# A cross-attention and graph kernel: the first batch's rows are loaded through another engine's queue, and earlier in it

## The chip, the cores and the metric

One Trainium2 chip, one core of it. The metric is the device time of one execution in microseconds (us). TensorE (PE) multiplies matrices, VectorE (DVE), ScalarE (ACT) and GpSimd (POOL) work on elements, and the sync engine (SP) issues transfers. ScalarE can issue transfers too. All transfers of a core are carried by the same 16 DMA engines; SP and ScalarE each feed them through a queue of their own (q1 and q10 in this profile).

## The reference

Four stages follow one another. Here they are in the program's terms, for 4 batches of 256 rows of 512:

```
# L0, an update of low rank, with a_sum made of the context's rows
w     = softmax(x @ router_W.T + router_b)              # 8 mixing weights per row
a_sum = sum over 4 of (x @ ctx.T)                       # 64 columns
x     = nan_to_num(x + 0.5 * sum_n w_n * (a_sum @ lora_B[n].T))
# L1, cross attention with a mask, 32 heads of 16, over the 64 rows of ctx
Q, K, V = x @ Wq.T + bq, ctx @ Wk.T + bk, ctx @ Wv.T + bv
x     = layernorm(x + softmax(mask(Q K.T / 4)) V @ Wo.T + bo) * ln_g + ln_b
# L2 and L3, each four blocks on a graph of the 8 nearest of 512 points
idx   = top_k(-distance(ctx), 8)
for block in range(4):
    p = leaky_relu(x)
    x = (w_c @ p + sum over neighbours of (w_n @ p)) / 9 + x   # w_c = w_n = fside
```

## The kernel before

Weights and x arrive with the contracted dimension first. x of one batch is a tile of 128 partitions by 4 chunks by 256 rows, loaded in two halves of two chunks (256 KB each, semaphores `x0_0` and `x0_1` for batch 0). Products that need precision are made of a high and a low part of each operand, so most operands are split by ScalarE (high part) and VectorE or GpSimd (low part) before TensorE uses them.

Each engine works through an order of steps written out by hand (PE_STEPS, ACT_STEPS, DVE_STEPS, POOL_STEPS, SP_STEPS), in which a step is a kind, a batch and an index. Engines wait for each other by semaphores only. An instruction that waits holds up everything behind it on its engine.

The transfers at the start are not in SP_STEPS. SP issues them in the order of the line LOADS, each through `load` (L442), ahead of all its other steps: mask, ctxT (the context with the contracted dimension first), x0, xyz0, loraB, wk, and so on. ScalarE's block begins with two small transfers of its own, the router's weights (`routerW`, L827, 16 KB) and the router's offset (`rb`, L829, 4 KB), and goes on with ACT_STEPS.

The steps near the start that matter here, by engine:
- VectorE: `fa` (the mask as numbers, and its counts, from `mask_all_i`), `a_ready` (the context's four row groups are added, L1143 and L1144), `fm` (ctx_m, the masked context), `near` (the 8 nearest of a stretch of the graph, L1152 and L1153), `rB` (mix, L1199), `ml` (mixT_lo, L1205).
- TensorE: after 28 warm-up products `lora0` (x_in by a_router; it waits for `a_ready`, `routerW` and each half of x0), `dist0_0`, `router0`, `dist0_1` to `dist0_3` (distances, from xyz and xyz_n), `keys` (ctx_m by wk, waits for `wk`), `adjT0` (L675), `mixed0` (L684), `dist1_0`, `lora1`, `dist1_1`, `ua0` (mixT by loraB).
- ScalarE: `sq0` (L834), `low0` (L872), `lbh` (loraB_hi), `rE0`, `wqh` (wq_hi, L840, waits for `wq`), `sq1` (L834, written to points), `adjC0`, `mh0_0` and `mh0_1` (mixT_hi, L882), `woh`.

Of the kernel before, what the change touches and what calls it, by code (L numbers as in the profile page):

```python
# [14 lines left out]
P = 128  # L15
B, S, H = 4, 256, 512
# [3 lines left out]
KC = H // P  # L20
# [17 lines left out]
BANK = 512  # L38
WARM_UP = 14
POOL_LN = ()  # L40
LOADS = "mask ctxT x0 xyz0 loraB wk xyz1 x1 small wq wv wo"

# [88 lines left out]
def xattn_graph_kernel(nc, xT, ctx, ctxT, mask, maskT, fsideT, lora_BT, router_WT, router_b,  # L133
# [28 lines left out]
    with stack:  # L162
# [6 lines left out]
        def under(*tensors):  # L169

            with ExitStack() as early:
                return [sb(name, shape, dt, early) for name, shape, dt in tensors]
# [23 lines left out]
        wk, wv = under(("wk", [P, KC, H], F32), ("wv", [P, KC, H], F32))  # L196
# [45 lines left out]
        def fb(name, shape, dt=F32):  # L242
            return sb(name, shape, dt, front)
# [4 lines left out]
        x_in = [fb(f"x_in{k}", [P, KC, S]) for k in range(2)]  # L248
# [9 lines left out]
        x1 = fb("x1", [P, KC, S])  # L258
# [5 lines left out]
        small = fb("small", [P, 8])  # L264
# [18 lines left out]
        loads = {}  # L283
# [156 lines left out]
        def _(sp):  # L440
            def load(dst, src, name):
                sp.dma_start(dst, src).then_inc(loads[name], 16)  # L442

            def chunks(w):
                return w.rearrange("(c p) n -> p c n", p=P)

            def load_x(b):
                src = xT.rearrange("(c p) (b s) -> b p c s", p=P, b=B)[b]
                for c in range(0, KC, 2):
                    load(x_in[b % 2][:, c:c + 2], src[:, c:c + 2], f"x{b}_{c // 2}")  # L450

            def load_xyz(b):
                load(xyz[b][0:V, :], ctx[b], f"xyz{b}")
                load(xyz_n[b][0:V, :], ctx[b], f"xyz{b}")

            def load_first(name):
                if name == "ctxT":
                    load(ctx_t[:], chunks(ctxT), name)
                elif name == "mask":
                    src = mask.rearrange("b v -> (b v)").unsqueeze(0).broadcast_to([P, B * V])  # L460
                    load(mask_all_i[:], src, "mask_all")
                elif name in ("x0", "x1"):
                    load_x(int(name[1:]))
                elif name in ("xyz0", "xyz1"):
                    load_xyz(int(name[3:]))
                elif name == "loraB":
                    load(loraB_raw[:], chunks(lora_BT), name)
                elif name == "wk":
                    load(wk[:], chunks(WkT), name)
                elif name == "wq":  # L470
                    load(wq_raw[:], chunks(WqT), name)
                elif name == "wv":
                    load(wv[:], chunks(WvT), name)
                    load(bv_all, bv.unsqueeze(0).broadcast_to([P, H]), "bv")
                    for half in range(2):
                        load(mask_col_i[half * V:(half + 1) * V, :], maskT, "mask_col")
                elif name == "wo":
                    load(wo_raw[:], chunks(WoT), name)
                    load(g_all[:], ln_g.unsqueeze(0).broadcast_to([P, H]), "ln")
                    load(b_all[:], ln_b.unsqueeze(0).broadcast_to([P, H]), "ln")  # L480
                elif name == "small":
                    load(bk_col[:], bk_cols, "bk")
                    load(bq_col[:], bq_cols, "bq")
                    sp.dma_start(bo_col[:], bo.rearrange("(c p) -> p c", p=P), allow_slow_non_contiguous=True)\
                        .then_inc(loads["bo_col"], 16)

            for name in LOADS.split():
                load_first(name)
# [335 lines left out]
        @block.scalar  # L824
        def _(act):

            act.dma_start(a_router[:, :, R:R + NE], router_WT.rearrange("(c p) n -> p c n", p=P))\  # L827
               .then_inc(loads["routerW"], 16)
            act.dma_start(rb_all[:], router_b.unsqueeze(0).broadcast_to([P, NE])).then_inc(loads["rb"], 16)  # L829
# [518 lines left out]
```

## Time and profile before

| | |
|---|---|
| median of 3 runs | 391.87 us (391.63 to 392.79) |
| the profiled execution's own time | 391.98 us |
| its span | 390.2 us |
| busy PE / PE weight loads | 372.0 us (95%) / 311.5 us (80%) |
| busy DVE | 279.2 us (72%) |
| busy ACT | 181.1 us (46%) |
| busy POOL | 127.6 us (33%) |
| moved by DMA | 22.60 MB, mean 58 GB/s |

The span runs from the first to the last instruction that the profiler recorded; 1.8 us of the execution's own time lie outside it. Busy shares are of the span. DMA shares in the tables are the mean busy share of the 16 DMA engines; values a little above 1 occur.

### The profile page before, as it was taken

Reading aid. Unit: us, or ns where it says so; the run is one execution under the profiler, and the core shown is the slowest. Engines: PE = TensorE matmul, PEld = TensorE weight load, DVE = VectorE, ACT = ScalarE, POOL = GpSimd, SP = SyncE. Lnnn points to the kernel's source line nnn. Section 1 sums busy time; section 2 is a strip of 40 time slices with the busy share of each in tenths; the row PEclk is TensorE's granted clock in tenths of the full one; section 3 lists DMA queues with packets and bytes.
Section 4 is the critical chain, followed back from the end, with each engine's and each line's share of the span. In section 5 each row is a group of like instructions: output and inputs, shape, how many; then the busy total and the mean of one; then the engine's idle time right before and its main releaser. Section 6 shows DMA issues by size and latency. Waiting matters only on the chain.

```text
span 390.2 us, 6603 instructions
## 1 busy us (share of the span) xinstructions
PE 372.0 (95%) x2428; PEld 311.5 (80%) x2428; DVE 279.2 (72%) x418; ACT 181.1 (46%) x308; POOL 127.6 (33%) x120
## 2 busy tenths in 40 slices
PE   5799997989999989998999999999999999999996
PEld 5476796776886866986869889888889889988995
DVE  5847859578679876676779877846777866786634
ACT  1357536748529776337735334333333334423410
POOL 7656020400200132203414745333435243523300
PEclk9999999999999999999999999999999999999999
DMA  7992416206435505300000000000000000000022
GB/s 176 299 380 77 127 38 149 61 2 125 86 110 125 113 2 114 89 7 2 2 2 2 0 0 2 0 2 2 0 3 0 2 0 0 3 2 0 2 108 108
DMA packets 25198, 22.60 MB, mean 58 GB/s; under 512 B 9552, under 2 KB 20688, under 8 KB 25168
## 3 DMA queue, kind: packets, MB, share of 16 engines
q1 hardware_dynamic: 24496, 22.17, 20.8%
q8 instruction: 20, 0.33, 0.4%
q10 hardware_dynamic: 672, 0.02, 0.1%
q14 instruction: 10, 0.08, 0.1%
HBM read 12.48 MB, written 3.15 MB: 40 GB/s over the span
## 4 chain that ended last, share of the span: by engine, by line
PE 80%; DMA 6%; DVE 4%; SPq 4%; ACT 3%; issue 2%; POOL 0%; ACTq 0%; DVEq 0%; POOLq 0%
PE slot L561 78%; DMA wk<-in_WkT 3%; SPq L493 2%; ACT probT L966 2%; DMA fs_raw<-in_fsideT 1%; DVE shift L1240 1%; DMA q_stack<-shiftT 1%; SPq L522 1%; SPq L442 1%; PE slot L684 1%; PE slot L675 1%; ACT L966 1%; DVE x L1223 1%; DVE x L1225 0%; PE slot L716 0%
## 5 line engine op out<-in xcount | busy, mean ns | idle before, releaser
L1055 POOL TENSOR_TENSOR p_lo<-p_full,p_hi 128x512 fp32r<-128x512 f32 x64 | 87.1, 1371 | 128.9 <-ACT p_hi L1006 128.8
L1006 ACT ACTIVATE p_hi<-p_full 128x512 fp32r<-128x512 f32 x64 | 39.9, 630 | 73.0 <-DVE p_full L1302 73.0
L561 PE MATMUL slot<-adj,u_hi 128*128 128x512 f32 x256 | 69.2, 395 | 0.0
L561 PE MATMUL slot<-adj,u_lo 128*128 128x512 f32 x256 | 68.5, 394 | 0.0
L1307 DVE TENSOR_TENSOR u_lo<-slot,u_hi 128x512 fp32r<-128x512 f32 x64 | 42.9, 686 | 34.5 <-ACT u_hi L1016 33.9
L1302 DVE SCALAR_TENSOR_TENSOR p_full<-points 128x512 f32<-128x512 f32 x64 | 63.1, 1003 | 3.3
L561 PE MATMUL slot<-fs_hi,p_hi 128*128 128x256 f32 x256 | 63.8, 283 | 0.5 <-ACT probT L966 0.5
L561 PE MATMUL slot<-fs_lo,p_hi 128*128 128x256 f32 x256 | 63.7, 282 | 0.0
L1312 DVE SCALAR_TENSOR_TENSOR points<-slot,points 128x512 f32<-128x512 f32 x64 | 43.5, 687 | 23.5 <-PE slot L561 23.3
L1016 ACT ACTIVATE u_hi<-slot 128x512 fp32r<-128x512 f32 x64 | 37.4, 597 | 44.2 <-PE slot L561 43.7
L561 PEld LDWEIGHTS slot<-adj,u_lo 128*128 128x128 f32 x256 | 45.9, 189 | 9.1 <-issue 1.3
L561 PEld LDWEIGHTS slot<-adj,u_hi 128*128 128x128 f32 x256 | 45.7, 188 | 8.7 <-issue 0.9
L561 PEld LDWEIGHTS slot<-fs_hi,p_hi 128*128 128x128 f32 x256 | 48.7, 190 | 2.0 <-ACT probT L966 1.0
L561 PEld LDWEIGHTS slot<-fs_lo,p_hi 128*128 128x128 f32 x256 | 48.7, 190 | 0.6
L561 PEld LDWEIGHTS slot<-fs_hi,p_lo 128*128 128x128 f32 x256 | 39.5, 189 | 6.7 <-issue 1.9
L561 PE MATMUL slot<-fs_hi,p_lo 128*128 128x256 f32 x256 | 44.2, 285 | 0.0
L1055 POOL TENSOR_TENSOR q_lo<-q_full,q_hi 128x512 fp32r<-128x512 f32 x8 | 10.4, 1308 | 76.0 <-DMA q_stack<-q_lo 53.6
L966 ACT ACTIVATE probT<-slot,mask_col 128x1024 f32<-128x1024 f32 x16 | 17.7, 1114 | 12.9 <-PE slot L561 12.9
L1240 DVE TENSOR_REDUCE shift<-slot 128x16 f32<-128x1024 f32 x16 | 19.3, 1216 | 5.4 <-PE slot L561 5.4
L1152 DVE MAX8 top<-slot 128x8 f32<-128x512 f32 x16 | 11.1, 695 | 10.0 <-PE slot L561 9.9
L933 ACT ACTIVATE k_blk_hi<-kT_hi,half_col 32x256 fp32r<-32x256 f32 x32 | 14.4, 497 | 1.8 <-PE slot L561 1.4
L561 PE MATMUL slot<-x_hi,wq_hi 128*128 128x256 f32 x64 | 14.2, 304 | 1.0 <-issue 1.0
(138 smaller groups left out, 567.5 us busy)
## 6 DMA issues: line engine op xcount, KB each, us to landing
q_stack<-q_hi SPq DMA_DIRECT2D x32, 128.0 KB, 2.8
x_in<-in_xT SPq DMA_DIRECT2D x8, 256.0 KB, 5.5
q_stack<-q_lo SPq DMA_DIRECT2D x16, 128.0 KB, 2.7
out_points<-points SPq DMA_DIRECT2D x8, 256.0 KB, 2.0
loraB_raw<-in_lora_BT SPq DMA_DIRECT2D x1, 1024.0 KB, 9.5
wk<-in_WkT SPq DMA_DIRECT2D x1, 1024.0 KB, 12.7
wq_raw<-in_WqT SPq DMA_DIRECT2D x1, 1024.0 KB, 10.8
wv<-in_WvT SPq DMA_DIRECT2D x1, 1024.0 KB, 11.6
```

The source lines that it names most:

```text
L493: sp.dma_start(q_stack[PART * part:PART * (part + 1), j::HC // 2, :].bitcast(F32), q[PART * j:PART * (j + 1)].bitcast(F32)).then_inc(signa ...
L561: return pe.matmul(dst, lhsT, rhs, start=start, stop=stop, skip_group_check=True)
L933: act.activation(k_blk_hi[rows, :, 2 * j + a, :], kT_hi[rows, :, b * V:(b + 1) * V].bitcast(F32), ACT.Copy, scale=half_col[rows, a:a + 1]) ...
L966: act.activation(probT[:, i % 2, :], both_banks("w", b, i)[:], ACT.Exp, bias=mask_col[:, b:b + 1], scale=QK_SCALE).then_inc(prob_ready, 1)
L1006: act.activation(p_hi[b][:, (i % 2) * H:(i % 2 + 1) * H], p_full[:, p_buf[b, i]], ACT.Copy)\
L1016: act.activation(half_of(u_hi[:, u], i % 2), bank("wa", b, i // 2, i % 2), ACT.Copy)\
L1055: pool.tensor_tensor(lo[:, cut], full[:, cut], hi[:, cut].bitcast(F32), ALU.subtract)\
L1152: link(dve.max(top8[:, i], tile))
L1240: dve.tensor_reduce(pairs, both_banks("sc", b, i)[:].rearrange("p (j a v) -> p j a v", a=2, v=V), AX_X, ALU.max, negate=True).then_inc(max ...
L1302: dve.scalar_tensor_tensor(p_full[:, p_buf[b, i]], pts, SLOPE, pts, ALU.mult, ALU.max)\
L1307: dve.tensor_tensor(half_of(u_lo[:, u], i % 2), bank("wa", b, i // 2, i % 2), half_of(u_hi[:, u], i % 2).bitcast(F32), ALU.subtract).then_ ...
L1312: dve.scalar_tensor_tensor(pts, bank("ga", b, i // 2, i % 2), 1.0 / (TOPK + 1), pts, ALU.mult, ALU.add).then_inc(points_ready, 1)
```

## The change

The two halves of x0 leave SP's list, and ScalarE's block issues them before its two router transfers. Same source, same destination, same sizes, same semaphores.

```diff
-LOADS = "mask ctxT x0 xyz0 loraB wk xyz1 x1 small wq wv wo"
+LOADS = "mask ctxT xyz0 loraB wk xyz1 x1 small wq wv wo"
...
-                elif name in ("x0", "x1"):
-                    load_x(int(name[1:]))
+                elif name == "x1":
+                    load_x(1)
...
         @block.scalar
         def _(act):
 
+            first_rows = xT.rearrange("(c p) (b s) -> b p c s", p=P, b=B)[0]
+            for c in range(0, KC, 2):
+                act.dma_start(x_in[0][:, c:c + 2], first_rows[:, c:c + 2]).then_inc(loads[f"x0_{c // 2}"], 16)
             act.dma_start(a_router[:, :, R:R + NE], router_WT.rearrange("(c p) n -> p c n", p=P))\
                .then_inc(loads["routerW"], 16)
             act.dma_start(rb_all[:], router_b.unsqueeze(0).broadcast_to([P, NE])).then_inc(loads["rb"], 16)
```

On SP, at the very start of the program, the issues stand as follows, with - what was there before and + what is there now (x_in is the tile of x0, xyz and xyz_n are the two copies of the first batch's context):

```order
 L442 DMA mask_all_i<-in_mask 128x256
 L442 DMA ctx_t<-in_ctxT 128x4x256
-L442 DMA x_in<-in_xT 128x2x256 x2
 L442 DMA xyz<-in_ctx 64x512
 L442 DMA xyz_n<-in_ctx 64x512
```

Two issues are gone, and everything behind them on SP moves up by two places.

On ScalarE, at the start of its block, these rows stood before (points holds the router's weights, as a_router):

```order
L824 UNCONDITIONAL_BRANCH
L827 DMA points<-in_router_WT 128x4x8
L829 DMA rb_all<-in_router_b 128x8
L834 ACT_TABLE_LOAD
L834 ACTIVATE xyz_n<-xyz_n 64x512
L872 ACTIVATE low<-slot 72x256
```

and these stand there now:

```order
L824 UNCONDITIONAL_BRANCH
L829 DMA x_in<-in_xT 128x2x256 x2
L830 DMA points<-in_router_WT 128x4x8
L832 DMA rb_all<-in_router_b 128x8
L837 ACT_TABLE_LOAD
L837 ACTIVATE xyz_n<-xyz_n 64x512
L875 ACTIVATE low<-slot 72x256
```

The two halves of x0 come first, and the router's weights and offset, the table load and `sq0` follow two issues later. Nothing else moves on any engine; line numbers behind the new lines are higher by 3.

## Rows read from the trace of the kernel before

**Rows 1.** The page: the span, and DMA's share in 40 slices.

```profile
span 390.2 us, 6603 instructions
...
DMA  7992416206435505300000000000000000000022
```

**Rows 2.** The chain of work that ended last: start us, us, what.

```profile
1.71 0.51 SPq L442
...
2.26 0.47 SPq L442
...
4.74 12.68 DMA wk<-in_WkT
...
17.46 7.17 PE slot L561 x32
...
25.53 0.88 PE slot L684 x8
```

**Rows 3.** The timeline, transfers being issued: start us, us, engine, line, out<-in.

```profile
0.80 0.46 ACTq L827 DMA_DIRECT2D points<-in_router_WT  x1
0.80 0.39 SPq L442 DMA_DIRECT2D mask_all_i<-in_mask  x1
...
1.29 0.52 ACTq L829 DMA_DIRECT2D rb_all<-in_router_b  x1
...
1.84 1.28 ACT L834 ACT_TABLE_LOAD   x1 [1.84 <-issue]
```

**Rows 4.** Windows: PE, PEld, DVE, ACT, POOL, PEclk, DMA share, GB/s.

```profile
1.00:2.00 1.00, 0.42 (x2) 0.42 (x3) 0.94 (x2) 0.16 (x1) 0.62 (x4) 1.00 0.06 17
2.00:3.00 1.00, 1.00 (x6) 1.00 (x6) 0.06 (x1) 1.00 (x1) 0.72 (x6) 1.00 0.39 65
3.00:4.00 1.00, 1.00 (x7) 1.00 (x6) 0.00 (x0) 0.12 (x1) 0.80 (x4) 1.00 0.67 85
4.00:5.00 1.00, 1.00 (x7) 1.00 (x7) 0.00 (x0) 0.00 (x0) 0.74 (x8) 1.00 0.93 200
...
16.00:17.00 1.00, 0.00 (x0) 0.00 (x0) 1.00 (x2) 0.00 (x0) 1.00 (x2) 1.00 1.10 207
```

**Rows 5.** DMA in short windows: transfers' us to landing, and a queue's packets.

```profile
ctx_t<-in_ctxT SPq DMA_DIRECT2D x1, 512.0 KB, 5.9
points<-in_router_WT ACTq DMA_DIRECT2D x1, 16.0 KB, 4.9
...
x_in<-in_xT SPq DMA_DIRECT2D x1, 256.0 KB, 7.4
...
q10 hardware_dynamic: 253, 0.01, 6.8%
```

**Rows 6.** The timeline ahead of keys: start us, us, engine, line, idle before.

```profile
5.53 0.98 DVE L1156 TENSOR_SCALAR attended<-mask_all_i 128x256 f32<-128x256 int32 x1 [3.41 <-DMA mask_all_i<-in_mask]
...
9.54 1.95 PE L561 MATMUL slot<-x_in,points 128*72 128x256 f32 x8 [2.94 <-DVE points L1144]
...
11.20 0.63 ACT L834 ACTIVATE xyz_n<-xyz_n 64x512 f32<-64x512 f32 x1 [8.07 <-DMA xyz_n<-in_ctx]
...
12.98 2.79 PE L561 MATMUL slot<-xyz_n,xyz 128*128 128x512 f32 x6
```

**Rows 7.** The timeline behind keys, from 20 to 30 us, on four engines.

```profile
20.95 1.41 DVE L1199 SCALAR_TENSOR_TENSOR mix<-slot,small,lge 128x512 f32<-128x512 f32 x2
...
23.18 1.91 ACT L840 ACTIVATE wq_hi<-wq_raw 128x2048 fp32r<-128x2048 f32 x1 [7.21 <-DMA wq_raw<-in_WqT]
...
25.11 0.63 ACT L834 ACTIVATE points<-points 64x512 f32<-64x512 f32 x1
...
26.25 1.02 PE L561 MATMUL slot<-points 128*128 128x512 f32 x2
...
28.72 1.28 DVE L1205 TENSOR_TENSOR mixT_lo<-slot,mixT_hi 128x512 fp32r<-128x512 f32 x2
...
29.62 0.39 PEld L561 LDWEIGHTS slot<-mixT_hi,loraB_hi 128*128 128x128 f32 x2 [0.47 <-DVE mixT_lo L1205]
```

## The prediction

> **What bounds the kernel now.** I read the chain of waits first, since only what lies on it can move the end. It starts with SP's issues, one behind the other, goes through the transfer of wk, issued at 4.74 us and landed 12.68 us later at 17.42, and then through TensorE: keys from 17.46, mixed0 at 25.53 [rows 2]. The two issues of x0 are links of that chain, 0.51 and 0.47 us long at 1.71 and 2.26. Next to 12.68 us of transfer the issues are small, so the second question is what the transfer waits for. The windows answer it: in the microseconds from 1 to 5 the DMA engines' share is 0.06, 0.39, 0.67, 0.93, and while wk is under way it is full, 1.10 at 16 to 17 us [rows 4]; the page's digits of 9 for the second and third slice (9.8 to 29 us) say that it stays so [rows 1]. wk therefore does not land a fixed time behind its issue. It lands when everything in front of it has been moved, and the same holds for wq, wv and wo behind it. The stretch of loads is limited by bytes, except for its first few microseconds, where the DMA engines lack work.
>
> Third, what lies beside the chain up to 30 us, as this says how much may come late and what must come early too. Ahead of keys, VectorE starts at 5.53 when the mask lands, and its chain (attended, left_out, counts, the sum of the context) releases lora0 at 9.54; the square of xyz_n starts at 11.20 when xyz_n lands; TensorE's last distances run from 12.98 for 2.79 us, to 15.77 [rows 6]. Then TensorE has nothing until 17.46: 1.69 us of slack. Behind keys, ScalarE sits idle 7.21 us until wq lands, makes wq_hi from 23.18 to 25.09 and the square for batch 1 from 25.11 to 25.74; TensorE's distances that read it start at 26.25, 0.51 us later; VectorE's mixT_lo at 28.72 releases the LoRA products at 29.62 [rows 7]. So between 17.46 and 29.62 two loads matter: wk directly, and wq by way of ScalarE, with 0.51 us of room. Behind 30 us the remaining loads are in or are issued by waits on other engines' work, and every start is relative to another: a shift at 29.62 is carried to the end one for one.
>
> **The change, part by part.** Removed from SP: two issues, 0.51 + 0.47 us with two pauses of 0.04, that is 1.06 us [rows 2]. xyz, xyz_n, loraB and wk are issued 1.06 us earlier, wk at 3.68. Added on ScalarE: two issues ahead of the router's two, whose own take 0.46 and 0.52 us, the first at 0.80 [rows 3]. So the halves of x0 are issued at about 0.80 and 1.31 rather than 1.71 and 2.26, and routerW, rb and the table load start some 1.0 us later. The table load moves from 1.84 to about 2.9 and ends near 4.2 (1.28 us) [rows 3]; ScalarE's first use of it is at 11.20 [rows 6], 7 us later, so this costs nothing. If the cover were gone it would cost 1.0 us of ScalarE.
>
> What 1.06 us of earlier issue is worth. The bytes don't change, and nor do their packets. Where the DMA engines are full, an earlier issue buys nothing; it buys the idle share that it fills. From 2 to 5 us that is 0.61 + 0.33 + 0.07 = 1.01 us of all 16 engines [rows 4]. That and the 1.06 us saved on SP are upper bounds for the gain at about the same value. The lower bound is 0: the mask and ctxT (640 KB) were issued by 1.67 us and still did not fill the engines from 2 to 4 us, so what kept them idle is not only a lack of issued work on q1. For a gain speaks that the other queue was moving in the same time, but only the router's pieces: 253 packets of together 0.01 MB from 2 to 4 us, 6.8% of the engines' time [rows 5]. In their place now stand x0's rows of 1 KB, real work. I take a little over half of 1.01 us: 0.6 us. By this, wk lands at 16.8 and wq 0.6 us earlier too, since both wait for the same backlog.
>
> What of it reaches the end. Keys start 0.6 us earlier, if TensorE is free (15.77, yes) and ctx_m is made. mixed0 would start at 24.9 instead of 25.53; the mix that it reads ends at 20.95 + 1.41 = 22.36 [rows 7], 2.5 us of room. The LoRA products start earlier by the smaller of wk's shift and wq's shift plus 0.51. With both at 0.6 it is 0.6. If only wk's landing moved, 0.51 us would be left.
>
> What comes later. x0 now shares the engines with mask and ctxT from the first microsecond. Before, ctxT took 5.9 us from issue to landing and the second half of x0 7.4 us, to 9.66 [rows 5]. If mask and ctxT come later, VectorE's chain slips, behind it lora0, the distances, the eight nearest, the mix. Room for that: 0.34 us in front of the first distances (lora0 ends at 9.54 + 1.95 = 11.49, they also wait for the square, which ends at 11.20 + 0.63 = 11.83 [rows 6]) plus 1.69 us in front of keys, about 2.0 us, or 1.4 us with keys 0.6 us earlier. I expect the mask to slip by less than 1 us: its 128 KB would yield to at most as much of x0, and 128 KB take 0.6 us at the 200 GB/s of 4 to 5 us, 1.5 us at the 85 GB/s of 3 to 4 [rows 4]. It costs nothing in the sum. The router's weights, now behind x0 in their queue, are needed at 9.54; they took 4.9 us before [rows 5]. Issued at about 1.85 they would land near 6.8 by that, and behind x0's last byte at 9 to 10 if they have to wait for it. That too is inside the room.
>
> Does sharing do anything but save issue time? The rows show only that q1 and q10 were both served from 2 to 4 us, the one with large packets, the other with small ones [rows 5]. The Trainium skill, "DMA: Bandwidth & Descriptors", section "Issuing engines are not separate DMA queues", says that transfers of several engines run on the same 16 DMA engines and interleave, and that issuing from more than one saves only the issuing engine's time. By that rule the gain is at most the issue time taken off SP, 1.06 us here; the trace agrees in so far as wk's landing is set by full engines. Its section "Queues, rings and completion order" says that each DMA engine takes its queues in turn, packet by packet; by that x0 would draw level with mask and ctxT and hold them up, which is the rival of a late lora0 below. No row here shows the turns.
>
> The sum: 391.98 us, the profiled execution's own time, minus 0.6 is 391.4. The profiled execution lies 0.11 us above the median of the runs, so against 391.87 the forecast is 391.3 us. Less than 0.3%, 1.2 us, is about what a measurement of this kernel can't tell from no change.
>
> **The rivals.**
> - *Nothing moves* (chance 0.23). The engines' idle share at 2 to 4 us comes from the start-up of transfers and not from missing issues. For it: 640 KB were issued and the share was 0.39. Against it: the second queue held only small pieces. wk lands at 17.4 as before: 391.9.
> - *The two queues together move faster* (0.14). The rate at full share is not constant: 207 GB/s at 16 to 17 us, and 200 at share 0.93 [rows 4]. If x0's rows mix better with others, wk could land 1.69 us earlier or more, until TensorE's own work ends at 15.77. wq would have to come 1.2 us earlier for it to pass ScalarE. Gain 1.2 to 1.7, about 390.4. Against it: that exceeds both upper bounds above, which hold at equal rates.
> - *lora0 comes late, slower* (0.08). The router's weights wait for the whole of x0, to 9.66, and then take their 4.9 us of before: 14.56. lora0 would start 5.0 us late and end at 16.5, behind it the distances and the router, 3.9 us as from 11.83 to 15.77 before, to 20.4, and keys would start at 20.4 instead of 17.46: 2.9 us later, 394.8. It decides from 2.0 us of lateness of lora0 on; a mask that late would do the same. Against it: most of the 4.9 us is start-up and the crowd of that moment, and the router's pieces cost the engines little.
> - *Only wk moves* (0.05, within the forecast's range): wq lands when it did, gain 0.5, 391.4.
>
> **How the numbers follow.** The forecast, a gain of 0.3 to 1.05, has 0.50: 390.8 to 391.6. With the smaller rivals around it, no change within 0.3% has 0.80, made of 0.50, 0.23, 0.05 and a small part of the third; faster by over 0.3% has 0.12, from the rival of the faster queues; slower by over 0.3% has 0.08. The range reaches from 390.3, which takes in most of the faster rival, to 392.4, which takes in no change with its scatter (the runs shown reach from 391.6 to 392.8); left out are the late lora0 and a tenth at most besides.
>
> **What would show it.** Right: in the profile after, SP's issue of wk starts near 3.7 us; DMA's share from 2 to 4 us is clearly above 0.39 and 0.67; wk lands at 16.4 to 17.1; wq_hi starts before 23.18 by a similar amount; the chain of waits still begins with SP, then wk; mixT_lo and the LoRA products are earlier by 0.3 to 1.0 us, and the same shift is seen late in the span. Wrong: a share from 2 to 4 us as before (then nothing moves), a lora0 later than 11.6, or keys that wait for anything but wk. The prediction also fails if the work behind 52 us, where VectorE enters the chain, does not carry the shift one for one.

## The result and the profile after

The change made the kernel slower: 395.88 us median of 6 runs (394.98 to 396.99) against 392.13 us for the kernel before in the same measurement (6 runs), a ratio of 1.0088 with a 95% interval of 1.0072 to 1.0104. Forecast was a small gain, 391.3 us, in a range up to 392.4. The profiled execution was the slowest of the six, 396.99 us with a span of 395.3; its mean granted clock was 0.983, that of the other five 0.990 or 0.991.

The page of the kernel after, its span, TensorE's share, its granted clock and DMA's share in 40 slices:

```profile
span 395.3 us, 6603 instructions
...
PE 376.6 (95%) x2428; PEld 315.5 (80%) x2428; DVE 279.8 (71%) x418; ACT 181.0 (46%) x308; POOL 127.9 (32%) x120
...
PEclk9699999898999999999999999999999999999999
...
DMA  6992426103504612600000000000000000000022
```

The same instructions ran (2428 products, 22.60 MB moved), yet TensorE was busy 4.6 us longer. The clock's row says why: it has a 6 in the second slice and an 8 in two later ones. The row of before had nines throughout:

```profile
PEclk9999999999999999999999999999999999999999
```

By the windows the fall in the second slice alone (0.60, 0.50, 0.50 and 0.69 from 10 to 18 us) makes a mean of 0.991 over the span. As an estimate from that, the other five executions had this fall and not the two later ones.

The chain of waits after (start us, us, what) begins in another place:

```profile
1.26 8.74 DMA ctx_t<-in_ctxT
...
10.03 0.70 DVE scratch L1146
...
10.75 0.44 DVE points L1147
11.19 2.52 issue
13.71 4.52 PE slot L561 x10
...
28.78 0.88 PE slot L684 x8
```

Before, it went through wk and then keys [rows 2]; now it goes through ctxT, VectorE's two sums and lora0. The 2.52 us called issue are a wait that this view doesn't name. mixed0 (L684) starts at 28.78 instead of 25.53, 3.25 us later. The timeline of the same stretch (start us, us, engine, line, idle before) shows the parts:

```profile
0.80 0.98 ACTq L829 DMA_DIRECT2D x_in<-in_xT  x2
...
1.81 0.49 ACTq L830 DMA_DIRECT2D points<-in_router_WT  x1
...
4.13 0.83 SPq L442 DMA_DIRECT2D wk<-in_WkT  x1
...
11.87 0.63 ACT L837 ACTIVATE xyz_n<-xyz_n 64x512 f32<-64x512 f32 x1 [6.72 <-DMA xyz_n<-in_ctx]
...
13.71 3.66 PE L561 MATMUL slot<-x_in,points 128*72 128x256 f32 x8 [6.17 <-issue]
...
20.81 7.07 PE L561 MATMUL slot<-ctx_m,wk 128*128 128x256 f32 x32
...
24.91 1.91 ACT L843 ACTIVATE wq_hi<-wq_raw 128x2048 fp32r<-128x2048 f32 x1 [4.95 <-DMA wq_raw<-in_WqT]
```

lora0 starts at 13.71 instead of 9.54 and takes 3.66 us instead of 1.95 [rows 6]. What it waited for is found in the DMA view (us from issue to landing), taken in short windows: the second half of x0, ctxT, the router's weights, wk, and last the packets of ScalarE's queue from 9.6 to 13.6 us:

```profile
x_in<-in_xT ACTq DMA_DIRECT2D x1, 256.0 KB, 8.3
...
ctx_t<-in_ctxT SPq DMA_DIRECT2D x1, 512.0 KB, 8.7
...
points<-in_router_WT ACTq DMA_DIRECT2D x1, 16.0 KB, 11.8
...
wk<-in_WkT SPq DMA_DIRECT2D x1, 1024.0 KB, 14.7
...
q10 hardware_dynamic: 170, 0.01, 3.2%
```

x0's second half was issued half-way through the 0.98 us from 0.80 and landed at about 9.6, where it landed before (9.66). ctxT landed at 10.0 instead of 7.2. The router's 16 KB, issued at 1.81, landed at 13.6, which is lora0's start: 11.8 us for a transfer that took 4.9 [rows 5]. wk, issued at 4.13, landed at 18.8 instead of 17.42. So with lora0 on time keys would still have begun 1.4 us late: of their 3.35 us, 2.0 lie beyond wk's landing. Windows (PE, PEld, DVE, ACT, POOL, PEclk, DMA share, GB/s):

```profile
2.00:3.00 1.00, 1.00 (x6) 1.00 (x6) 0.06 (x1) 0.00 (x0) 0.72 (x6) 1.00 0.13 40
3.00:4.00 1.00, 1.00 (x7) 1.00 (x6) 0.00 (x0) 0.14 (x1) 0.80 (x4) 1.00 0.48 165
4.00:5.00 1.00, 1.00 (x7) 1.00 (x7) 0.00 (x0) 1.00 (x1) 0.75 (x8) 1.00 0.72 249
...
7.00:12.00 5.00, 0.54 (x5) 0.35 (x3) 3.25 (x8) 0.13 (x1) 4.43 (x7) 0.84 1.09 218
...
12.00:13.00 1.00, 0.00 (x0) 0.00 (x0) 0.96 (x2) 0.50 (x1) 0.66 (x1) 0.50 1.06 376
```

More bytes were moved from 3 to 4 us than before (165 GB/s, was 85), but the engines' share from 2 to 5 us fell, from 0.39, 0.67 and 0.93 to 0.13, 0.48 and 0.72 [rows 4]. From 7 to 12 us fewer bytes were moved at an unchanged share. Before, the same stretch reads:

```profile
7.00:12.00 5.00, 2.02 (x9) 1.17 (x9) 4.79 (x10) 0.78 (x2) 4.43 (x7) 1.00 1.07 276
```

218 GB/s were moved instead of 276, so 0.1 MB more from 2 to 5 us was followed by 0.3 MB less. Of the packets of this stretch 451 had under 512 bytes, before 58, and ScalarE's queue took 12.2% of the engines' time. Why full engines move fewer bytes isn't shown. And TensorE's clock, after TensorE had stood still since 7.5, was granted at 0.50, the lower of its two levels (1.2 of 2.4 GHz).

### The profile page after: what moved, and what is told of

Same layout as the page of the kernel before. It is cut to its first block, busy times and chain, and to the rows that moved or that the text cites. A ratio compares the mean times of both kernels' runs of the same rounds, so it can differ in the third digit from the quotient of the medians.

```text
span 395.3 us, 6603 instructions
## 1 busy us (share of the span) xinstructions
PE 376.6 (95%) x2428; PEld 315.5 (80%) x2428; DVE 279.8 (71%) x418; ACT 181.0 (46%) x308; POOL 127.9 (32%) x120
## 2 busy tenths in 40 slices
DMA packets 25198, 22.60 MB, mean 57 GB/s; under 512 B 9552, under 2 KB 20688, under 8 KB 25168
## 3 DMA queue, kind: packets, MB, share of 16 engines
q10 hardware_dynamic: 1216, 0.55, 0.5%
## 4 chain that ended last, share of the span: by engine, by line
PE 83%; DMA 5%; SPq 3%; DVE 3%; ACT 3%; issue 2%; POOL 0%; ACTq 0%; DVEq 0%; POOLq 0%
PE slot L561 81%; DMA ctx_t<-in_ctxT 2%; SPq L493 2%; ACT probT L969 1%; DMA fs_raw<-in_fsideT 1%; DMA q_stack<-shiftT 1%; SPq L522 1%; PE slot L675 1%; PE slot L684 1%; DVE shift L1243 1%; ACT L969 1%; DVE x L1228 0%; PE slot L716 0%; ACT fs_hi L993 0%; DVE x L1226 0%
## 5 line engine op out<-in xcount | busy, mean ns | idle before, releaser
L561 PE MATMUL slot<-x_hi,wq_hi 128*128 128x256 f32 x64 | 15.0, 318 | 1.0 <-issue 1.0
## 6 DMA issues: line engine op xcount, KB each, us to landing
loraB_raw<-in_lora_BT SPq DMA_DIRECT2D x1, 1024.0 KB, 11.2
```

Source lines behind the costliest of these rows:

```text
L561: return pe.matmul(dst, lhsT, rhs, start=start, stop=stop, skip_group_check=True)
```

## Experiments

Ratios are to the kernel before, in the runs of the same measurement. Spans and starts are of one profiled execution each; before's is 390.2 us.

**1. The router's weights first.**

```diff
+            act.dma_start(a_router ...routerW)
+            act.dma_start(rb_all ...rb)
             for c in range(0, KC, 2):
                 act.dma_start(x_in[0][:, c:c + 2], ...)
-            act.dma_start(a_router ...routerW)
-            act.dma_start(rb_all ...rb)
```

> The changed kernel with ScalarE's four issues in another order: router's weights, router's offset, then the two halves of x0. Theory A (the loss is the router's pieces standing behind x0 in their queue): the weights land near 6 us as before, lora0 starts when ctxT and VectorE allow, near 11.2 instead of 13.7; the distances end before wk lands (18.8), keys start near 18.9 instead of 20.8; time 2 to 3 us below the changed kernel, near 393.5. Theory B (the loss is x0 sharing the engines from the start, whatever the router does): lora0 and keys start as in the changed kernel, time near 395.9.

Measured: 392.64 us, ratio 0.9983 (0.9964 to 1.0002), span 391.3. The loss is gone. The timeline:

```profile
9.70 1.05 PE L561 MATMUL slot<-x_in,points 128*72 128x256 f32 x4 [3.11 <-DMA x_in<-in_xT]
...
11.66 1.86 PE L561 MATMUL slot<-x_in,points 128*72 128x256 f32 x4 [0.90 <-DMA x_in<-in_xT]
...
17.87 7.07 PE L561 MATMUL slot<-ctx_m,wk 128*128 128x256 f32 x32
```

The router's weights landed 4.7 us after their issue, as before. lora0 began at 9.70, earlier than theory A had it, since more than the weights changed: x0 is now issued behind ctxT, which landed at 7.65 instead of 10.0, and VectorE's sums were done by 9.5. So this run takes away two causes at once, the late weights and the late ctxT; theory B, in which the order on ScalarE does nothing, is out. Now x0 is the late one; its second half landed at 11.6, 2.0 us later than from the sync engine's queue, though issued within 0.1 us of the same time. wk, issued at 3.69, landed 13.2 us later at 16.9, 0.5 us earlier than before. That would be the gain that the prediction had named, but in run 7, with the same loads, wk landed at 17.4; a difference of 0.5 us is what two profiles of the same loads show. lora0's split and a clock of 0.50 in part of 12 to 16 us held TensorE, and keys began 0.4 us later than before.

**2. 28 warm-up products instead of 14**, all else as in the change. The numbers are those of WARM_UP; the trace counts two products for each.

> The changed kernel with 28 warm-up products instead of 14, so that TensorE is busy until about 13.5 us and has no gap in front of lora0. Theory A (part of the loss is TensorE's clock, granted at 0.5 from 10.3 to 17.1 us after TensorE stood still from 7.5 to 13.7): the clock stays at 1.00, lora0 takes 1.95 us instead of 3.66, keys start near 18.9 (wk's landing), time 1.7 to 2.5 us below the changed kernel. Theory B (the clock is a side effect, keys wait for something else): lora0 is shorter but keys start at 20.8 as before and the time is that of the changed kernel, 395.9. If the clock also falls later (68 and 92 us) because of the early gap, these falls vanish too; if not, they stay.

Measured: 395.91 us, ratio 1.0065 (1.0037 to 1.0092). The test needed a busy TensorE until 13.5 us, and the number of products was mis-sized:

```profile
1.58 8.81 PE L561 MATMUL slot<-ident 128*128 128x128 f32 x56 [1.58 <-POOL ident L1027]
...
13.18 3.60 PE L561 MATMUL slot<-x_in,points 128*72 128x256 f32 x8 [2.79 <-issue]
```

The products ended at 10.4, 2.8 us stayed empty, and lora0 took 3.60 us all the same. Inconclusive on the clock; repeated as 6.

**3. The router's weights laid out in memory as one row of 128 bytes for each partition.** This was to give the transfer 128 pieces instead of 512. The tile that it writes stays as it was, with the router's 8 columns at the end of each of 4 chunks, 32 bytes at a time.

```diff
-            act.dma_start(a_router[:, :, R:R + NE], router_WT.rearrange("(c p) n -> p c n", p=P))\
+            act.dma_start(a_router[:, :, R:R + NE], router_WT)\
...
-        "router_WT": a["L0_xattn_router_W"].T,
+        "router_WT": a["L0_xattn_router_W"].T.reshape(KC, P, NE).transpose(1, 0, 2),
```

> The changed kernel with the router's weights laid out in memory as one row of 128 bytes for each partition, so that the transfer has 128 pieces instead of 512. Order of issues unchanged. Theory A (the weights are late because many small pieces behind x0 wait their turn between full-sized pieces of the other queue): they land at least 1.5 us earlier than 13.6, near 10 to 11.5, and lora0 starts with ctxT's chain, near 11.2. Theory B (the lateness is a fixed start-up or x0's place in front): they land near 13 us or later, and the time stays at 395.9.

Measured: 396.30 us, ratio 1.0071 (1.0048 to 1.0094). From issue to landing, and the packets of the whole profile:

```profile
points<-in_router_WT ACTq DMA_DIRECT2D x1, 16.0 KB, 11.5
...
DMA packets 25198, 22.60 MB, mean 57 GB/s; under 512 B 9552, under 2 KB 20688, under 8 KB 25168
```

11.5 instead of 11.8 us, but the page of the change has the same 25198 packets, 9552 of them under 512 bytes, and the same 1216 in ScalarE's queue. The new layout did not lessen the pieces, so this run tests neither theory, and whether fewer pieces would land earlier stays open. It is of use as a second kernel that runs like the change.

**4. The router's transfers held back, x0 left with the sync engine** (kernel before).

```diff
+            loaded(act, "ctxT")
             act.dma_start(a_router[:, :, R:R + NE], router_WT.rearrange("(c p) n -> p c n", p=P))\
```

> The kernel before, with ScalarE's two router transfers issued only once ctxT has landed (7.2 us), x0 staying with the sync engine. Nothing stands in front of the router's pieces in their queue. Theory A (pieces of 32 bytes are slow whenever the other queue keeps the engines full): from issue to landing 4 us or more, landing at 11.5 or later, lora0 late by 2 us or more. Theory B (they are slow only behind x0 in the same queue): landing within 2.5 us, at 9.7, lora0 about as before and time 392.1.

Measured: 399.58 us, ratio 1.0166 (1.0124 to 1.0208). The timeline's lora0:

```profile
16.49 3.30 PE L561 MATMUL slot<-x_in,points 128*72 128x256 f32 x8 [9.60 <-DMA points<-in_router_WT]
```

The DMA view of 10 to 11 us, in which ScalarE's queue is absent as from 7 us on, that of 11 to 12 us, in which it appears for the first time, and the transfer's time to landing:

```profile
q1 hardware_dynamic: 177, 0.36, 102.9%
...
q1 hardware_dynamic: 197, 0.39, 104.2%
q10 hardware_dynamic: 38, 0.00, 2.4%
...
points<-in_router_WT ACTq DMA_DIRECT2D x1, 16.0 KB, 9.4
```

Issued at 6.99 with nothing ahead of it in its queue, the transfer moved no packet before 11 us and landed at 16.4. So it isn't x0 in front that it takes: this transfer was late with nothing in front of it, while the other queue kept the DMA engines full (103 to 109% from 7 to 12 us). That the sync engine's queue would have been faster at that moment isn't shown: wk, issued there at 4.65, landed at 17.5, behind this transfer.

**5. The router's transfers in the sync engine's queue, behind x0** (kernel before).

```diff
-LOADS = "mask ctxT x0 xyz0 loraB wk xyz1 x1 small wq wv wo"
+LOADS = "mask ctxT x0 router xyz0 loraB wk xyz1 x1 small wq wv wo"
...
+                elif name == "router":
+                    load(a_router[:, :, R:R + NE], router_WT..., "routerW")
+                    load(rb_all[:], router_b..., "rb")
```

> The kernel before, with the router's two transfers issued by the sync engine right behind x0, and none by ScalarE. The pieces are the same 640 small ones, behind the same x0, but in the queue that carries the large transfers. Theory C (what is late is the second queue, which gets little of full DMA engines): the weights land near 9.9 us, just behind x0's second half, lora0 starts at 10 to 10.5, keys with wk near 18, time 392 to 393. Theory D (small pieces are late in either queue once the engines are full): they land at 12 us or later, and lora0 with them, time 394 or more.

Measured: 392.54 us, ratio 0.9984 (0.9970 to 0.9997).

```profile
points<-in_router_WT SPq DMA_DIRECT2D x1, 16.0 KB, 7.2
```

Issued at 2.77, later than in the change, the same 512 pieces behind the same x0 landed at 9.97, and lora0 started at 10.01. Theory C holds: neither x0 ahead nor small pieces are enough to make the weights late, and in the second queue they are. Whether small pieces are delayed more there than large ones, no run separates; x0's large halves took 1.1 and 1.9 us longer there in run 1.

**6. 43 warm-up products**, all else as in the change.

> The changed kernel with 43 warm-up products, enough to last until about 13.5 us (28 lasted only until 10.4, and TensorE's clock was still granted at 0.5 from 13 to 17 us). Theory A (the clock is a part of the loss of its own): no 0.5 before 20 us, lora0 takes 1.95 us, keys start at wk's landing, 18.4 to 18.9, time 1.7 to 2.4 us below the changed kernel, 393.5 to 394.2. Theory B: keys start at 20.2 to 20.8 all the same and the time stays at 395.9.

Measured: 393.76 us, ratio 1.0023 (1.0008 to 1.0037), span 392.0, clock 1.000 for the whole span.

```profile
13.61 1.89 PE L561 MATMUL slot<-x_in,points 128*72 128x256 f32 x8
...
18.95 7.07 PE L561 MATMUL slot<-ctx_m,wk 128*128 128x256 f32 x32
```

lora0 is as late as in the change and keys begin 1.9 us earlier. The change's ratio was 1.0088 in its own measurement; with the gap filled 0.65 points of it are gone, some 2.5 us. That compares two measurements; runs 2 and 3, which kept the clock's fall, stood at 1.0065 and 1.0071 in a third, and against them it is 0.4 to 0.5 points, 1.7 to 1.9 us. The rest, 0.23% or 0.9 us, goes with keys that start 1.5 us late. It isn't all lora0's: wk landed at about 18.4 in this profile, so some 0.9 us of the 1.5 would be there with lora0 on time.

The kernel before doesn't keep its clock in every execution either. In the measurement of runs 5 to 8 its mean granted clock was 0.999 or 1.000 in 8 of 31 executions and 0.987 to 0.996 in the others; here it was 0.999 or 1.000 in 9 of 10, in the change 0.983 to 0.991 in all six. Against the median of those 8, 392.65 us, this kernel is 1.1 us slower.

**7. As 1, with 25 warm-up products.**

> The kernel of router first, x0 behind it on ScalarE's queue, with 25 warm-up products so that TensorE is busy until about 9.6 us. In that kernel wk landed at 16.9, 0.5 us earlier than before, but lora0 was split by a wait for x0's second half (11.6 us) and the clock fell to 0.5 from 12 to 15 us. If the clock is what ate the gain: no 0.5 before 20 us, lora0's second half at 11.7, the distances end near 16.6, keys start at 16.9 to 17.0, time 0.4 to 1.0 us below the kernel before. If not: within 0.3 us of the kernel with 14 products.

Measured: 393.34 us, ratio 1.0006 (0.9983 to 1.0029), span 390.4, clock 1.000. The clock was kept, but wk landed at 17.4 in this execution instead of 16.9, and keys began at 17.41. The expected lead did not show: wk's landing at 16.9, on which it rested, was not seen again.

**8. x0 alone on ScalarE's queue;** the router's transfers lead the sync engine's list.

```diff
-LOADS = "mask ctxT xyz0 loraB wk xyz1 x1 small wq wv wo"
+LOADS = "router mask ctxT xyz0 loraB wk xyz1 x1 small wq wv wo"
```

> x0 alone on ScalarE's queue, issued there from 0.80 us as in the change; the router's two transfers go to the sync engine, ahead of the mask. This leaves of the change only x0's move. If the whole loss is the router's late weights: they land near 6 us, lora0 starts with ctxT's chain near 11 to 11.5, keys near 18, time within 1 us of the kernel before. If x0's sharing with mask and ctxT costs by itself: ctxT lands at 10 us or later, lora0 no earlier than 12, keys at 19 or later, time 1.5 us or more above before.

Measured: 394.86 us, ratio 1.0049 (1.0026 to 1.0072), span 392.6. The timeline, from the mask's first use on:

```profile
8.20 1.28 DVE L1159 TENSOR_SCALAR attended<-mask_all_i 128x256 f32<-128x256 int32 x1 [6.08 <-DMA mask_all_i<-in_mask]
...
11.96 3.69 PE L564 MATMUL slot<-x_in,points 128*72 128x256 f32 x8 [4.64 <-DVE points L1147]
...
19.71 7.07 PE L564 MATMUL slot<-ctx_m,wk 128*128 128x256 f32 x32
```

Here x0 is what arrived early: its halves landed by 4.2 and about 6.1 us. The mask landed at 8.2 instead of 5.5, through it VectorE released lora0 at 11.96 (ctxT, landed at 10.7, was just in time for the sums at 10.76), and the clock was at 0.50 once more. About 1.0 us of that is the mask's later issue, behind the router's two. The rest is in the time from issue to landing, which the later issue doesn't touch: 6.3 us for the mask instead of 4.7, 8.4 us for ctxT instead of 5.9. So x0, issued from the start in the other queue, costs ctxT 2.5 to 2.8 us, here as in the change (8.7 us), and lora0 needs all three. The mask's 6.3 us is not shown to be x0's doing, as it took 4.8 in the change: here it also had the router's pieces ahead of it and was issued 1.0 us behind x0. Keys began at 19.71 and the time was 1.7 us above before, as expected if x0's sharing costs by itself; the late weights are not the whole loss.

**9. wk before loraB, wq before x1** (kernel before).

```diff
-LOADS = "mask ctxT x0 xyz0 loraB wk xyz1 x1 small wq wv wo"
+LOADS = "mask ctxT x0 xyz0 wk loraB xyz1 wq x1 small wv wo"
```

> The kernel before with two pairs of the sync engine's list exchanged: wk ahead of loraB, wq ahead of x1 and the small ones. Nothing on ScalarE's queue changes. This tests the path of the prediction by itself (wk, then wq with 0.51 us of room, shift what comes after one for one). If the path is as stated: wk lands near 13.6, keys start at 15.8 when TensorE is free, wq lands near 20.5, the LoRA products start near 28.0 instead of 29.6, and the time is 1.4 to 1.7 us below before, ratio 0.996. Rival (something else binds within 1 us, as the late low part of loraB or VectorE's nearest neighbours): gain below 0.7 us.

Measured: 392.42 us, ratio 0.9985 (0.9970 to 1.0001), span 390.7. The timeline:

```profile
15.98 7.07 PE L561 MATMUL slot<-ctx_m,wk 128*128 128x256 f32 x32
...
28.28 0.57 PE L561 MATMUL slot<-mixT_hi,loraB_hi 128*128 128x256 f32 x2
...
30.23 1.91 ACT L850 ACTIVATE adj<-wo_raw 128x2048 fp32r<-128x2048 f32 x1 [2.72 <-DMA wo_raw<-in_WoT]
...
32.56 0.32 PE L660 MATMUL slot<-ident,low 72*128 72x72 f32 x2 [1.08 <-ACT low L872]
```

Keys began 1.5 us earlier and the LoRA products 1.4 us earlier, as the path said. Then the lead was given back: ScalarE stood 2.72 us for wo, `low1` is behind it in ScalarE's order, and TensorE waited 1.08 us for `low1`. A third load, wo, stands on the path with about 1 us of room (before, `low` ends at 31.65 and is read at 32.58); here it was issued at 22.85 instead of 20.83 and landed at 30.2 instead of 29.4. The prediction had not named it. By 43 us the lead was 0.1 us, and the rival of this run, something else within 1 us, holds.

**10. The order of 9 with x0 on ScalarE's queue, as in 1.**

> The same new order of the sync engine's list, with x0 on ScalarE's queue behind the router's two transfers (the kernel of router first). x0 then lands at 11.6 us or later, since the second queue is served late while the engines are full. If that lateness is what counts once wk is early: lora0's second half waits for x0, the distances end near 16.6 to 18, and the gain of the new order is lost by half or more against the same order with x0 on the sync engine; time between 391.5 and 393. Rival (x0's queue doesn't matter, only the bytes ahead of wk): as fast as the kernel with the new order alone, or 0.5 us faster.

Measured: 392.85 us, ratio 1.0001 (0.9977 to 1.0024), span 391.1. lora0 began at 9.59 but took 3.62 us at the low clock, and keys began at 16.65, 0.7 us later than in 9. Further on, windows of this kernel:

```profile
64.00:68.00 4.00, 4.00 (x27) 3.95 (x26) 3.83 (x9) 3.21 (x8) 0.00 (x0) 0.57 0.21 51
88.00:92.00 4.00, 4.00 (x35) 1.47 (x34) 3.57 (x7) 3.43 (x7) 0.00 (x0) 0.58 0.44 98
```

In these two falls of the clock went a lead of 0.9 us that it had at 43 us (in its chain of waits, TensorE's run of 64 products starts at 42.72; 43.63 before). The gain of 9 was lost, as expected, but not in the expected way: lora0 shows no wait for x0's second half. And as 9 had gained only 0.6 us, the two intervals overlap.

**11. As 5, with 26 warm-up products.**

> The kernel with the router's two transfers on the sync engine behind x0, now with 26 warm-up products, so that TensorE is busy until about 9.5 us. That kernel's profile had the clock at 0.5 in part of 10 to 14 us and lower again between 80 and 100. If the clock costs wherever a gap of more than 3 us stands ahead of lora0: clock 1.00 all through, lora0 1.95 us long, span 390.0 to 390.5 instead of 391.4, time 0.5 to 1 us below 392.54. Rival (falls come by chance and the early gap has no part in them): time as without the products, 392.5, and a fall somewhere in the profile.

Measured: 393.58 us, ratio 1.0013 (0.9984 to 1.0041), span 392.6. A clear miss:

```profile
9.97 1.92 PE L564 MATMUL slot<-x_in,points 128*72 128x256 f32 x8 [0.86 <-issue]
...
17.88 8.86 PE L564 MATMUL slot<-ctx_m,wk 128*128 128x256 f32 x32 [1.99 <-DMA wk<-in_WkT]
```

lora0 ran at the full clock, but after the 1.99 us in front of keys the clock fell: from 18 to 22 us it was granted at 0.57 to 0.58, and keys took 8.86 us instead of 7.07. The profile of before stands still for 1.69 us in the same place [rows 6] and keeps its clock.

**12. As 10, with 26 warm-up products.**

> The kernel with the new order of the sync engine's list and x0 on ScalarE's queue behind the router's transfers, now with 26 warm-up products. Its profile without them was 0.9 us ahead of before at 43 us and lost this to a lower clock from 60 to 100 us. If the clock is what took it: clock 1.00 all through, the lead of 0.9 us or a little more is kept to the end, span 389.0 to 389.6, time 0.9 to 1.5 us below before (ratio 0.996 to 0.998). Rival (the lead is given back to another wait, as that for wo): span 390 or more, ratio 0.999 or more.

Measured: 393.17 us, ratio 1.0007 (0.9985 to 1.0029), span 391.9. The clock stayed at 1.00 and keys began at 16.77. But the chain of waits shows where the lead went:

```profile
23.60 8.30 DMA wo_raw<-in_WoT
...
33.74 0.37 ACT low L875
...
34.25 0.32 PE slot L660 x2
```

wo landed at 31.90, and the router's transposes of batch 1 began 1.7 us later than in 9. The rival (given back to the wait for wo) holds for this profile. That of run 10, with the same loads, had wo issued at 20.99 and landed at 28.7, and wq landed at 20.6 instead of 23.2: between two profiles of the same loads such landings differ by 2 to 3 us, and what differs isn't shown.

No kernel tried beats the one before by more than about 0.2%; 5 is the only one whose interval leaves out no change, and barely.

## Why the prediction was wrong

- **The bound was read rightly, but not all of it.** Keys waited for wk and the LoRA products for wq, and run 9, with both loads earlier, moved keys by 1.5 and the LoRA products by 1.4 us. "A shift at 29.62 is carried to the end one for one" failed in that run: wo, by way of `low1`, has about 1 us of room.
- **The issue times were right, the share was not.** xyz was issued 1.06 us earlier. But both queues' issues became longer (the router's offset took 1.51 us, xyz_n 1.01), so that wk was issued at 4.13, 0.61 us earlier instead of 1.06. It landed at 18.8, not at 16.8, and 0.8 to 1.0 us later than before in runs 2, 3 and 6 too. The DMA engines' share from 2 to 4 us, which was to rise above 0.39 and 0.67, was 0.13 and 0.48. So the term of 0.6 us in the sum was a loss of 1.4 us at wk: "The bytes don't change", but at full share they moved at 218 instead of 276 GB/s from 7 to 12 us. With the router's pieces in front wk landed at 16.9 (run 1) and 17.4 (run 7), a gain of 0.5 us or none.
- **The step that failed** is the bound on the router's weights: "Issued at about 1.85 they would land near 6.8 by that, and behind x0's last byte at 9 to 10 if they have to wait for it. That too is inside the room." They landed at 13.6. The duration of 4.9 us had been read before the DMA engines were full (shares of 0.06 to 0.93 from 1 to 5 us [rows 4]); the rival that named 4.9 us on top of x0's landing came to 14.56, 1 us off. The change and run 5 show that the place matters: behind the same x0, issued at 1.81 in the second queue, the transfer landed at 13.6; issued at 2.77 in the sync engine's, at 9.97, within the bound of the prediction. Run 4 shows that x0 ahead isn't needed for a landing 9.4 us after the issue.
- **ctxT was taken to be free.** "I expect the mask to slip by less than 1 us": it slipped by 0.1, but ctxT by 2.8 us, and VectorE's sums with it, to 11.2. This alone would have kept lora0 until 11.2. It lies inside the 2.0 us of room, and the router's weights covered it.
- **The price of a late lora0 was mis-sized.** The rival gave 2.9 us for 5.0 us of lateness, at full clock. Measured were 4.2 us of lateness and 3.35 us at keys. The missing term is the clock: 3.66 - 1.95 = 1.7 us in lora0 alone. Sum: 4.17 + 1.71 - 2.0 of room = 3.9, against the measured 3.35; 0.4 us of the difference is that in the timeline the distances start 0.2 us ahead of lora0's end and keys 0.2 us ahead of theirs. Run 6, which fills the gap and leaves the lateness, takes 0.88% down to 0.23%. It also has none of the later falls. In the change's profile they are at 68 to 72 and 92 to 96 us (0.57 each), and 5.1 - 3.25 = 1.85 us of the span's growth arise behind mixed0, where they are. This execution is 1.1 us above the median of its kernel, so in a usual one less than that arises there.
- **The chances.** The rival "lora0 comes late, slower" was the right mechanism and got 0.08. Against it stood "the router's pieces cost the engines little". Before, all 672 packets of ScalarE's queue had moved by 7 us, in which they took 5.3% of the engines' time; in the change 467 of its packets fell into 7 to 12 us and took 12.2%, which is 0.6 us of all 16 engines (an estimate, with some of x0's rows among them). And the argument says nothing of when the pieces' turn comes.
- The Trainium skill's rule that issuing from several engines saves only the issuing engine's time ("DMA: Bandwidth & Descriptors", "Issuing engines are not separate DMA queues") bounds the gain at 1.06 us, and no run here exceeds it at wk (0.5 us in run 1, none in run 7, 1.05 from run 9 to run 10); it does not tell of wk's 1.4 us of loss in the change, nor of the worse place in the second queue. By the Trainium skill's account of turns between queues, packet by packet ("DMA: Bandwidth & Descriptors", "Queues, rings and completion order"), packets that waited in the second queue would have moved between those of the first. In run 4 none moved for 4 us; the measurement decides, and whether they were waiting there yet no run shows.

Still open: what keeps the second queue waiting. It could be the preparation of transfers in a common line, or the way in which full engines choose. Run 4 excludes that it takes something ahead in the same queue, and run 5 that small pieces behind x0 are late in any queue; run 3 was to exclude the number of pieces and left it as it was. Open is also why wk landed later. Open too is when exactly the clock falls. Nine of the fourteen profiles have a fall that begins ahead of 20 us, in each case during or behind a stretch in which TensorE stood still, in run 11 of only 1.99 us; but 2.94 us in front of lora0 and 1.69 us in front of keys brought none in the profile of before, an execution with a clock of 1.000 such as only 8 of 31 came near.

## What to carry to other kernels

The time from issue to landing of a small transfer, read before the DMA engines are full, did not hold for the same transfer once a queue had filled them (4.9 us, then 11.8): what an early product needs is issued first, ahead of anything large, in either queue. Before a load is moved forward, list all that its first reader needs, as the room is that of the last to arrive; here lora0 waited for the context's sums before, for the router's weights in the change and for x0 in run 1. And a wait on TensorE early in a kernel is to be priced twice, by its length and by the clock after it, and a lead won in a stretch of loads is kept only if every later load on the path has moved too. An edit that is to change how a transfer is cut up is checked in the count of packets, and a difference of 0.5 us at one landing asks for a second profile of the same loads.

## What was not expected of the hardware

- A transfer of 16 KB issued from ScalarE at 6.99 us, behind nothing in its queue, moved its first packet after 11 us and took 9.4 us, with the sync engine's queue at 103 to 109% of the DMA engines.
- x0's halves, issued from ScalarE at 1.86 to 3.06 us (run 1), landed at about 9.6 and 11.6; from the sync engine at 1.71 and 2.26 they landed at 8.3 and 9.7.
- Profiles with a fall of the clock that begins ahead of 20 us had further ones between 64 and 132 us in five of nine cases (after, runs 2, 4, 5 and 10). The five without an early fall (before, runs 6, 7, 9 and 12) had none. These are one execution of each kernel.
- At a share of 1.07 to 1.09 the DMA engines moved 276 GB/s from 7 to 12 us before and 218 in the change.
